# One-hot places by one broadcast comparison, and score keys and prologue contexts as 128-column stationaries

## The reference

```python
x = x + tanh(g_xattn) * xattn(layernorm(x), ctx, ctx)
x = x + tanh(g_ffn) * ffn(layernorm(x))

# xattn: H = 16 heads of DK = 32
Q = (query @ Wq.T + bq) ; K = (key @ Wk.T + bk) ; V = (value @ Wv.T + bv)     # split into heads
attn = softmax(Q @ K^T / sqrt(DK)) ; out = attn @ V
expert = mean over e of (out @ We[e].T + be[e]) ; return expert @ Wo.T + bo

# ffn: E = 8 experts, C = 100 places each
probs = softmax(hs @ w_gate) ; best = argmax(probs) ; gate = probs[best]
mask = one_hot(best) ; locations = cumsum(mask, axis=0) - 1
mask = mask * (locations < C) ; loc_oh = one_hot(sum(locations * mask), C)
dispatch / combine by mask x loc_oh ; expert_out = dispatched @ w_expert + b_expert
```

## Time and profile before

| | |
|---|---|
| median of 3 runs | 406.76 us |
| profiled execution | 407.26 us |
| its span | 405.5 us |
| TensorE busy | 398.0 us (98%), 3102 matmuls |
| VectorE busy | 336.7 us (83%) |
| ScalarE busy | 225.7 us (56%) |
| GpSimd busy | 167.0 us (41%) |
| granted TensorE clock | full, over the whole span |

### The profile page before, as it was taken

How to read it: one execution, slowest core, us unless ns; L and a number is a source line. 1 busy time by engine, 2 the same in 40 slices (tenths; PEclk the granted TensorE clock), 3 DMA queues, 4 the chain that set the end, 5 groups by cost and what they waited for, 6 DMA issues and landing times.

```text
span 405.5 us, 8725 instructions
## 1 busy us (share of the span) xinstructions
PE 398.0 (98%) x3102; PEld 190.1 (47%) x3102; DVE 336.7 (83%) x683; ACT 225.7 (56%) x320; POOL 167.0 (41%) x155
## 2 busy tenths in 40 slices
PE   8999999999999999999999999999999999899996
PEld 5556664444444444444444444444444444354444
DVE  7448666986898989988998999899897689779996
ACT  5434523568556763946585485748556464776110
POOL 2026999324181157309033530813261064460371
PEclk9999999999999999999999999999999999999999
DMA  7999991464059307824950692295169016241585
GB/s 271 318 386 394 345 387 60 103 125 151 2 128 208 147 13 162 222 86 91 189 202 1 150 229 103 64 181 191 47 133 242 3 34 173 80 136 27 97 174 178
DMA packets 65901, 63.19 MB, mean 156 GB/s; under 512 B 42277, under 2 KB 45617, under 8 KB 65859
## 3 DMA queue, kind: packets, MB, share of 16 engines
q1 hardware_dynamic: 60747, 56.19, 50.4%
q0 software_dynamic: 1632, 3.49, 3.1%
q10 hardware_dynamic: 3480, 2.96, 2.2%
HBM read 29.59 MB, written 12.98 MB: 105 GB/s over the span
## 4 chain that ended last, share of the span: by engine, by line
PE 85%; DVE 7%; issue 4%; ACT 2%; DMA 1%; POOL 0%; SPq 0%; DVEq 0%; ACTq 0%
PE ps L840 68%; PE ps L456 9%; PE ps L588 3%; PE ps L405 2%; DVE xb L1567 2%; DVE bn_raw L1573 1%; DVE place_hot L1724 1%; DMA raw<-in_L_xattn_Wk_dram 1%; ACT probs L1234 1%; DVE part_lo L1625 1%; ACT mixT_hi L397 0%; PE ps L1161 0%; DVE mixT_lo L398 0%; POOL known L1930 0%; PE ps L606 0%
## 5 line engine op out<-in xcount | busy, mean ns | idle before, releaser
L1234 ACT ACTIVATE probs<-ps 120x1024 f32<-120x1024 f32 x64 | 62.0, 1023 | 20.9 <-PE ps L840 20.8
L1602 DVE TENSOR_REDUCE neg_max<-ps 128x16 bf16<-128x1920 f32 x32 | 68.8, 2149 | 3.6 <-PE ps L840 3.6
L1989 POOL TENSOR_TENSOR attn_lo<-attn,attn_hi 128x512 f16<-128x512 f32 x28 | 31.8, 1158 | 91.6 <-ACT attn_hi L1234 91.6
L840 PE MATMUL ps<-xnT_hi,wqT_hi 128*128 128x512 f16 x128 | 48.6, 380 | 0.0
L840 PE MATMUL ps<-mixT_hi,attn_hi 128*128 128x512 f16 x128 | 48.5, 379 | 0.0
L840 PE MATMUL ps<-mixT_lo,attn_hi 128*128 128x512 f16 x128 | 48.5, 379 | 0.0
L840 PE MATMUL ps<-xnT_lo,wqT_hi 128*128 128x512 f16 x128 | 48.5, 379 | 0.0
L1997 POOL TENSOR_TENSOR xb<-xb,mix_bias 128x512 f32<-128x512 f32 x32 | 39.6, 1268 | 14.2 <-DVE cb_col L1544 14.2
L1234 ACT ACTIVATE q_hi<-ps,bias_cols 128x512 f16<-128x512 f32 x32 | 22.0, 689 | 31.5 <-PE ps L840 31.5
L840 PE MATMUL ps<-q_stack,k_stack 97*120 97x512 f16 x128 | 34.6, 388 | 1.4 <-ACT probs L1234 1.0
L840 PE MATMUL ps<-probs,den_sel 120*32 120x256 f32 x512 | 34.1, 384 | 0.0
(11 more groups left out here) (278 smaller groups left out, 803.7 us busy)
## 6 DMA issues: line engine op xcount, KB each, us to landing
xb<-in_x_dram SPq DMA_DIRECT2D x8, 1024.0 KB, 6.1
q_stack<-q_hi SPq DMA_DIRECT2D x48, 128.0 KB
out_dram<-xb SPq DMA_DIRECT2D x6, 1024.0 KB, 7.2
raw<-in_L_xattn_We_dram SPq DMA_DIRECT2D x5, 1024.0 KB, 12.4
q_stack<-q_lo SPq DMA_DIRECT2D x32, 128.0 KB
xb<-in_L_xattn_We_dram SPq DMA_DIRECT2D x3, 1024.0 KB, 10.8
k_stack<-k_scratch SPq DMA_DIRECT2D x8, 360.0 KB, 4.4
k_scratch<-k_hi ACTq DMA_DIRECT2D x16, 120.0 KB, 7.0
```

The lines of the kernel that those rows point to most:

```text
L840: return e.matmul(out_, a, b, start=start, stop=stop, **kw)
L1234: return e.activation(out_, in_, func, **kw)
L1602: e.tensor_reduce(maxed[:, :, :, g], quad[:, :, 0:NT * SK].rearrange("p j (t s) -> p t j s", t=NT), AX.X, ALU.max, negate=True).then_inc(s ...
L1989: e.tensor_tensor(attn_lo[:, g, :], attn[:, g, :], attn_hi[:, g, :], ALU.subtract).then_inc(s_alo, 1)
```

## The change

Three edits, with no change to the order of the work.

- `enter_places` does one comparison over all four tiles, with `place_iota` and `place` both broadcast, instead of four.
- `k_stack`'s slot becomes one run of 4 x 480 columns with 8 more at its end, and `scores` takes 128 columns from the first key of a head group on: the 120 keys and the 8 that follow them in memory. The result fills all 128 partitions; the last 8 are not read. GpSimd clears the 8 extra columns and writes the constant row over them too; TensorE waits for both.
- The value projections of batches 0 to 6 take 128 columns of the turned context and write 128 partitions, of which 120 are read as before.

```diff
-        k_stack = sb("k_stack", [P, 2, HJ, NK * SK], F16)
+        k_stack = sb("k_stack", [P, 2, HJ * NK * SK + P - SK], F16)
...
-                return (ctxT_hi, ctxT_lo)[p][:, k, b_ * SK:(b_ + 1) * SK]
+                return (ctxT_hi, ctxT_lo)[p][:, k, b_ * SK:b_ * SK + P]
...
-                return products3(e, b[0:SK, :], rows_of, lambda p, k: (mixT_hi, mixT_lo)[p][:, k, :])
+                return products3(e, b[0:SK, :] if b_ == B - 1 else b, rows_of, lambda p, k: (mixT_hi, mixT_lo)[p][:, k, :])
...
-                    load(k_stack[0:3 * DK, slot, :, :], k_scratch[r + 1], s_ks[slot])
+                    load(k_stack[0:3 * DK, slot, 0:HJ * NK * SK], k_scratch[r + 1].rearrange("d j s -> d (j s)"), s_ks[slot])
...
-                    e.wait_ge(s_set, SET + 2)
+                    e.wait_ge(s_set, SET + 4)
...
-                    ins = mm(quad[0:SK, j, :], k_stack[0:STACK, b % 2, j, g * SK:(g + 1) * SK],
-                             q_stack[0:STACK, j, g, :])
+                    first = (j * NK + g) * SK
+                    ins = mm(quad[:, j, :], k_stack[0:STACK, b % 2, first:first + P], q_stack[0:STACK, j, g, :])
...
-                for t in range(NT):
-                    ins = e.tensor_scalar(place_hot[:, t, :], place_iota[:, :], place[:, t:t + 1], None, ALU.is_equal)
-                ins.then_inc(s_en, 1)
+                e.tensor_tensor(place_hot[:, :, :], place_iota[:, :].unsqueeze(1).to_broadcast([P, NT, CAP]),
+                                place[:, :].unsqueeze(2).to_broadcast([P, NT, CAP]), ALU.is_equal).then_inc(s_en, 1)
...
-                made_const(e.memset(k_stack[3 * DK:STACK, i, :, :], SHIFT_UNIT))
+                made_const(e.memset(k_stack[3 * DK:STACK, i, :], SHIFT_UNIT))
+                made_const(e.memset(k_stack[0:3 * DK, i, HJ * NK * SK:], 0.0))
```

## The result

| | before | after |
|---|---|---|
| median on one chip, 7 runs each | 406.78 us (406.39 to 407.17) | 405.47 us (404.88 to 406.70) |
| ratio after / before | | 0.9964, 95% interval [0.9955, 0.9974] |
| profiled execution, its span | 407.26 us, 405.5 us | 405.64 us, 403.9 us |

The change makes the kernel 0.36% faster: 1.5 us, with an interval of 1.1 to 1.8. That is above the 0.2% that I set as the border. 405.47 lies 0.4 us above the forecast of 405.05 and inside the range of 404.3 to 406.4, but 0.07 outside the narrower 404.8 to 405.4 that I gave for the likeliest case.

A forecast was written before the change was run, and what follows sets the result against it. TensorE, busy 98%, was taken as the bound, VectorE next at 83%. Terms 0.52 + 0.10 + 0.06 + 0.80 + 0.23 = 1.71 us off gave 405.55 profiled, 405.05 median, range 404.3 to 406.4.

The forecast's parts named there:

- the likeliest case: The forecast itself holding, with all its terms: chance 0.66, median 404.8 to 405.4 us.
- Loads and cold groups: Score matmuls right behind a 32-column group, their first load unhidden: 128-column keys save 0.035 us per such group.
- Rival A: The 97-row, 128-column load is not fast, so wider keys and contexts give nothing: 405.7 us, chance 0.07.
- Which cold groups count: 15 groups on TensorE's path, three before the first batch's value sums end, two in each of six following batches: 0.52 us.
- Batch 0's three cold groups: Score groups before the first batch's value sums are done, counted as on TensorE's path at 0.035 us each.
- The places: One comparison of 0.57 us frees TensorE's table earlier; capped by the exponentials, 0.20 us per batch, 0.80 in four.
- Rival B: Comparison no faster than four, or its gain stops at another wait: 0.8 us gained, 405.95 us, chance 0.12.
- The last batch: VectorE's chain from the places to the last scores is the path; places 0.24 us shorter gain 0.23 us.
- the pair that is cold again: Last batch's two scores after waiting for exponentials, at 352.80: 0.035 us saved, one of three such counted, 0.10 together.
- The contexts: Seven prologue value projections with 128-column stationaries; only two start with an unhidden load: 0.06 us together.
- Rival C: TensorE's stall for score shifts' DMA landing comes back before other batches: one 405.5 us, two 406.0, chance 0.07.

The follow-up runs named there:

- the kernel with the short exponentials: Changed kernel with ScalarE's second half of head group 0's exponentials cut from two heads to one from batch 1 on; 405.19 us, ratio 0.9963.
- the layout alone: Changed kernel with four comparisons and 120-column contexts and keys, leaving only k_stack's longer slots and the two memsets; 407.03 us, ratio 1.0004.
- the two last versions: Changed kernel, last statistics ahead of one-hot places, table ahead of scores: 412.34 us; second also reads places ahead of statistics: 405.46 us, ratio 0.9954.

## Why the prediction was right, point by point

- **Loads and cold groups.** Right in mechanism and size: 98 ns, and 0.037 per cold group where I took 0.035. Rival A is out; the 127-column kernel shows what it would have been.
- **Which cold groups count.** The one term that failed. Batch 0's three cold groups were to give 0.105 and gave nothing (+0.012). Their gain went into a wait a few microseconds later. Waits of TensorE's queue from 98.2 to 99.3 us, before and then after:

```profile
PEld ps L840 <- ACT part_x L1234: 0.5, 1, 0.5
```

```profile
PEld ps L840 <- ACT part_x L1234: 0.6, 1, 0.6
```

  The first gate sums wait for `part_x`, for which ScalarE's turn comes at 98.07 and at 98.37, and TensorE's lead of 0.11 is gone there. I had taken every cold group ahead of a batch's value sums as on the path, without following batch 0 to its next wait. In batches 1 to 6 there is no such wait, and 0.105 forecast stand against 0.103 and 0.118 in batches 1 and 2.
- **The places.** The comparison took 0.568 us (0.57 from the line through the earlier trace rows). A batch gained 0.262 to 0.264 where 0.27 was forecast, capped by the exponentials as said: the third matmul stands 0.05 behind them, and the kernel with the short exponentials shows that 0.07 more was to be had. Rival B (a comparison no faster, or a gain that stops at another wait) is out but for this cap.
- **The last batch.** From its last tile of x on, the places end 0.24 earlier, and the transposes and the last matmul 0.28 earlier (0.543, less the 0.266 by which that tile itself is early). Forecast: 0.23 for the places and 0.035 for the pair that is cold again.
- **The contexts.** 0.067 of the prologue, 0.06 forecast; the same in all twelve traces, by the width of their contexts.
- **The sum.** 1.61 us of mechanism against 1.71 forecast; without batch 0's term it would have been 1.6. The ratio gives 1.5, its interval 1.1 to 1.8. That the two profiled executions differ by 1.6 is in part luck: 0.37 less in waits and 0.36 more ahead of the first weights happened to cancel.
- **Rival C.** TensorE's waits at first scores come and go, and they do stand for the landing of the score shifts, which I had only argued. In the twelve traces 34 of the 84 first scores behind batch 0 waited, and each of them started 0.35 or 0.44 us behind the landing of its shifts; the 50 that did not wait started 0.38 to 0.83 behind it. Summed over the eight batches of one execution each, the waits are 0.53 us before, 0.41 with the contexts alone and 1.18 with the comparison alone, all three with the old slots of `k_stack`; with the new slots 0.21 after, 0.21 with the layout alone and 1.61 with the keys alone. Both layouts show small and large sums, so the moved tiles are not what makes them.
- **What such a wait costs.** Before the change, a batch that began late took part of it back, because TensorE waited for VectorE's places anyway: with the contexts alone, batch 4 began 0.11 late and took 36.109 instead of 36.217; before, batch 2 began 0.54 late and was 0.14 shorter than the batches after it. After the change, batch 4 began 0.17 late and took 35.952, as long as the others, so there the same wait costs in full. Whether the shorter batches also make such waits more likely is not shown: in batches 3 to 7 they sum to 0.00, 0.03, 0.29 and 0.38 us in the four kernels with batches of 36.2 us or more and to 0.13 to 1.16 in the eight with shorter ones, one execution each. With that, where the last 0.1 or 0.2 us between the 1.61 and the ratio went stays open.

## What to carry to other kernels

Where a 16-bit stationary is a few columns short of 128, see what follows it in memory: here the load took 137 ns at 127 columns and 98 at 128, and this paid only in groups that the matmuls before them do not cover. Follow each gain on to the next wait on the same engine before counting it; here it held in every batch but the one with such a wait, and in the loop it was cut at the exponentials. Where executions differ by 0.5 us through waits on landings, compare piece by piece with those waits taken off: that told 0.07 us apart where the medians could not. Check first that the wait is not taken up by another engine's queue, and count from that engine's instruction where it is: the second of the two last versions looked ahead of the kernel after from one starting point and was behind from the other.

## What the runs showed of the hardware that was not expected

- A broadcast comparison with both operands in float32 takes 568 ns for 128x400. When a second one was put ahead, it took 575 ns, and the batch grew by 0.54.
- TensorE's waits at the first scores of a batch, which end 0.35 or 0.44 us behind the landing of SyncE's DMA of the score shifts, were between 0 and 0.77 us, in kernels whose order around them is the same. That DMA took 0.08 us longer in the nine traces with the longer slots of `k_stack` than in the three with the old ones.
- One order of VectorE's last lists took some 7 us more in the median of six executions. In the one that was traced, signals from TensorE came 2 to 5 us behind their records, and TensorE stood 4.1 us and then ran at a clock of 0.50 for some 6 us. A neighbouring order had none of it.
